# Linear attention and feed-forward kernel: size checks moved ahead of the division, a buffer for the gated row, later weight words, projection banks in the last attention group

## The reference

```python
h = _layernorm(x) * (1 + ca) + sa
x = x + ga * attention(h, W_qkv, b_qkv, W_out, b_out)
h = _layernorm(x) * (1 + cb) + sb
x = x + gb * ffn(h, w_gate, w_up, w_down)

# attention, one row t after the other, per head
q = elu(q * E ** -0.5) + 1.0001
k = elu(k) + 1.0001
kv_s = kv_s + k_t outer v_t
k_s  = k_s + k_t
out_t = (q_t . kv_s) / (q_t . k_s + 1e-6)

# ffn, with integer weights (-127 to 127) times 1/127
h = silu(x @ w_gate.T) * (x @ w_up.T)
return h @ w_down.T
```

## Time and profile before

| What | us |
|---|---|
| median of 3 runs | 2218.9 (2216.57 to 2219.52) |
| profiled execution, whole | 2216.51 |
| its span, first to last instruction | 2214.8 |
| TensorE busy | 2134.8 (96%) |
| VectorE, ScalarE, GpSimd busy | 1212.1, 828.3, 834.9 |
| one pair of attention groups in the loop | 132.5 |
| `out_project`, twelve matmuls, start to start | 2.72 |
| `numerators`, start to end | 2.05 |
| `scores`, `k_turn`, `add_state` | 1.1, 0.43, 0.4 |
| one feed-forward block j, gate and up | 3.63 |
| transposes of group g+1 behind a block | 0.44 |
| TensorE's wait ahead of 69.72, in the first group | 2.33 |

### The profile page before, as it was taken

The page is one execution under the profiler, slowest core; times in us unless marked ns, Lnnn a source line. Parts: engine busy times, 40 slices in busy tenths (PEclk is TensorE's granted clock), DMA queues, the critical chain, the costliest instruction groups (busy, mean ns, idle before and its releaser), DMA issues. The chain is left out here.

```text
span 2214.8 us, 39000 instructions
## 1 busy us (share of the span) xinstructions
PE 2134.8 (96%) x15216; PEld 1746.5 (79%) x15216; DVE 1212.1 (55%) x1702; ACT 828.3 (37%) x1389; POOL 834.9 (38%) x630
## 2 busy tenths in 40 slices
PE   6999999999999999999789999999999999999999
PEld 4788788778778787788678888888888888888887
DVE  7988888888888888888532223322233322333211
ACT  5544444444444444445432233322233212332221
POOL 2633544443544443544333233333333323333333
PEclk9999999999999999999989999999999999999999
DMA  6111211211211211211511100111000111001100
GB/s 242 39 49 49 72 45 59 73 59 58 73 44 61 70 58 63 68 44 58 206 58 39 38 15 25 38 38 38 18 25 33 38 38 38 9 28 38 38 20 20
DMA packets 61079, 117.38 MB, mean 53 GB/s; under 512 B 5137, under 2 KB 5137, under 8 KB 60946
## 3 DMA queue, kind: packets, MB, share of 16 engines
q1 hardware_dynamic: 60418, 114.32, 14.9%
q10 hardware_dynamic: 528, 1.05, 0.1%
HBM read 81.80 MB, written 33.56 MB: 52 GB/s over the span
## 5 line engine op out<-in xcount | busy, mean ns | idle before, releaser
L1203 POOL TENSOR_TENSOR h_lo<-bv_row,h_hi 128x512 fp32r<-128x512 f32 x96 | 124.2, 1293 | 311.3 <-ACT h_hi L1262 311.3
L721 DVE RECIPROCAL r_den<-r_den 128x512 f32<-128x512 f32 x64 | 214.0, 3344 | 0.0
L1203 POOL TENSOR_TENSOR h_lo<-k_sum,h_hi 128x512 fp32r<-128x512 f32 x96 | 123.9, 1291 | 180.4 <-ACT h_hi L1262 180.4
L376 POOL TENSOR_TENSOR x_res<-a_t,x_res 128x512 f32<-128x512 f32 x64 | 81.9, 1280 | 281.3 <-DVE a_t L745 281.2
L1259 ACT ACTIVATE kv_diag<-pj 128x512 f32<-128x512 f32 x96 | 56.5, 588 | 343.3 <-PE pj L1358 343.3
L499 ACT ACTIVATE z_exp<-pj,qk_neg 128x512 f32<-128x512 f32 x128 | 88.1, 688 | 209.5 <-PE pj L958 173.1
L1262 ACT ACTIVATE h_hi<-bv_row 128x512 fp32r<-128x512 f32 x96 | 60.7, 632 | 263.6 <-DVE bv_row L1319 263.6
L726 DVE TENSOR_TENSOR probs<-sc,causal 128x512 f32<-128x512 f32 x256 | 158.4, 680 | 0.9 <-PE sc L986 0.8
L958 PE MATMUL pj<-xt_hi,w_hi 128*128 128x512 f32 x512 | 149.5, 413 | 4.7 <-ACT xt_hi L491 3.5
L1319 DVE TENSOR_TENSOR k_sum<-pj,kv_diag 128x512 f32<-128x512 f32 x96 | 66.4, 692 | 154.5 <-PE pj L1358 116.2
L1370 PE MATMUL num<-wd,h_hi 128*128 128x512 f32 x384 | 149.4, 389 | 0.0
(11 more groups left out here) (172 smaller groups left out, 4934.2 us busy)
## 6 DMA issues: line engine op xcount, KB each, us to landing
x_res<-in_L_attn_x SPq DMA_DIRECT2D x64, 256.0 KB, 2.9
x_mid<-x_res SPq DMA_DIRECT2D x64, 256.0 KB, 2.0
out<-y_rows SPq DMA_DIRECT2D x64, 256.0 KB, 2.0
xg<-in_L_attn_x SPq DMA_DIRECT2D x15, 1024.0 KB, 5.5
word<-in_ffn_words SPq DMA_DIRECT2D x36, 256.0 KB, 2.7
xg<-x_mid SPq DMA_DIRECT2D x9, 1024.0 KB, 5.6
r_den<-x_mid SPq DMA_DIRECT2D x8, 1024.0 KB, 5.7
wd_words<-in_ffn_words SPq DMA_DIRECT2D x12, 256.0 KB, 6.1
```

What stands on the lines that cost most here:

```text
L376: pool.tensor_tensor(out=x_res[:, slot, :], in0=y[:, :], in1=x_res[:, slot, :], op=ALU.add).then_inc(y_ready, 1)
L721: dve.reciprocal(r_den[parity][:, c, :], r_den[parity][:, c, :]).then_inc(rden_ready, 1)
L1203: pool.tensor_tensor(out=h_lo[j], in0=h[j % 2], in1=h_hi[j].bitcast(F32), op=ALU.subtract).then_inc(h_lo_ready, 1)
```

## The change

- `y` is a buffer of its own; `divide` no longer waits for `y_ready`. The two buffers of `word` lie in parts of `r_den`; the first load of a group waits for the divisions of the group before.
- In the loop `word_size` stands ahead of `divide`, and ScalarE waits for the third check behind the last `a_high`.
- The last group's `k_turn` goes to the first bank of `pj` and waits for `v_rows` in place of two masked heads; the projections of tiles 59 to 62 go to the second bank and wait for the gating before.
- SyncE issues the `up` words one tile later, and all of the group-15 words behind the residual load of tile 63, with the feed-forward part's groups 1 and 0 ahead of them (`first_group`). `gb_row` stays behind the last store.
- ScalarE converts the wide words in group 15 only, and the last thirds and the down words inside the first feed-forward group, which is a branch of its own now. TensorE starts that group after 8 conversions and waits for the other 8 at block 8.

The diff's core. The repeats of the `word_size` move at the other two tiles, and lines that pass a name on, are left out.

```diff
@@ -187,8 +188,7 @@
-    y = a_t
-    word = sbuf(s, "word", [P, D])
+    y = sbuf(s, "y", [P, D])
...
@@ -244,14 +244,23 @@
-    silu_row, junk = a_t, word
-    gb_row, ga_sign = a_t, word
+    silu_row, junk = a_t, y
+    gb_row, ga_sign = a_t, y
+    word = [r_den[1 - parity][:, 3, :].bitcast(I32) for parity in range(2)]
+    def turn_bank_of(tile):
+        return pj[:, 0, :] if isinstance(tile, int) and tile >= (NG - 1) * GT else turn_bank
+    def y_bank_of(tile):
+        return pj[:, 1, :] if isinstance(tile, int) and (NG - 1) * GT <= tile + 1 < NG * GT else y_bank
-    def sync(sp):
+    def sync(sp, first_group):
...
@@ -268,10 +277,12 @@
 
-        def load_word(i):
+        def load_word(g, parity, t):
+            i = g * 3 + (t - 6)
+            if t == 0:
+                wait(sp, a_ready, g * GT)
             wait(sp, most_ready, i + 1)
-            sp.dma_start(word[:, :].bitcast(I32), ffn_words[bass.ds(i, 1), :, :].rearrange("a p n -> (a p) n")).then_inc(word_in, 16)
+            sp.dma_start(word[parity], ffn_words[bass.ds(i, 1), :, :].rearrange("a p n -> (a p) n")).then_inc(word_in, 16)
 
...
@@ -324,21 +335,21 @@
+                if isinstance(g, int) and g == NG - 1 and t == 3:
+                    first_group()
+                    load_rest(words_hi, 0, 2)
+                    load_rest(words_lo, HB, 3)
+                    for j in range(HB):
+                        sp.dma_start(wd_words[:, j, :], ffn_words[2 * HB + j, :, :]).then_inc(words_in[4 + j // C], 16)
-                    load_word(g * 3 + (t - 6))
+                    load_word(g, parity, t)
+                if isinstance(g, int) and g == NG - 2 and t == 3:
-                if isinstance(g, int) and g == NG - 1 and t == 0:
-                    sp.wait_ge(pj_ready, NG * UNITS)
-                    load_rest(words_hi, 0, 2)
-                    load_rest(words_lo, HB, 3)
-                    sp.wait_ge(state_ready, (NG - 1) * GT)
-                    for j in range(HB):
-                        sp.dma_start(wd_words[:, j, :], ffn_words[2 * HB + j, :, :]).then_inc(words_in[4 + j // C], 16)
...
@@ -514,7 +525,7 @@
-            act.activation(k_tok[:, :], turn_bank, ACT.Copy).then_inc(ktok_ready, 1)
+            act.activation(k_tok[:, :], turn_bank_of(tile), ACT.Copy).then_inc(ktok_ready, 1)
...
@@ -599,13 +603,13 @@
-            if last:
-                words_to_float(w_lo, words_lo, slice(0, 2 * D), 1)
+            if last:
+                words_to_float(w_hi, words_hi, slice(0, 2 * D), 0)
...
@@ -615,12 +619,12 @@
-            if last:
-                words_to_float(w_hi, words_hi, slice(2 * D, 3 * D), 2)
+            if last:
+                words_to_float(w_lo, words_lo, slice(0, 2 * D), 1)
...
@@ -631,28 +635,23 @@
-            if last:
-                words_to_float(w_lo, words_lo, slice(2 * D, 3 * D), 3)
-                down_to_float(range(0, C))
-            if isinstance(g, int) and g == NG - 2:
-                words_to_float(w_hi, words_hi, slice(0, 2 * D), 0)
-            if last:
-                down_to_float(range(C, HB))
-            else:
+            if not last:
+            if not isinstance(g, int):
+                act.wait_ge(most_ready, g * 3 - 2)
...
@@ -732,7 +731,6 @@
-            wait(dve, y_ready, tile)
...
@@ -742,7 +740,7 @@
-            dve.tensor_tensor(out=y[:, :], in0=y_bank, in1=ga_row[:, :],
+            dve.tensor_tensor(out=y[:, :], in0=y_bank_of(tile), in1=ga_row[:, :],
...
@@ -750,10 +748,10 @@
 
-        def word_size(i, slot):
+        def word_size(i, slot, parity):
 
             wait(dve, word_in, i * 16 + 16)
-            dve.tensor_reduce(most[:, slot:slot + 1], word[:, :].bitcast(I32), AX.X, ALU.max,
+            dve.tensor_reduce(most[:, slot:slot + 1], word[parity], AX.X, ALU.max,
                               apply_absolute_value=True).then_inc(most_ready, 1)
...
@@ -868,9 +866,9 @@
+            if not isinstance(g, int):
+                word_size(g * 3 + (0 - 6), 0, parity)
-            if not isinstance(g, int):
-                word_size(g * 3 + (0 - 6), 0)
...
@@ -988,9 +986,12 @@
         def k_turn(tile, parity, t):
-            wait(pe, probs_ready, tile * HPC + 2)
+            if isinstance(tile, int) and tile >= (NG - 1) * GT:
+                pe.wait_ge(v_ready, NG * C)
+            else:
+                wait(pe, probs_ready, tile * HPC + 2)
             for c in range(C):
-                mm = pe.transpose(turn_bank[:, c * P:(c + 1) * P], kt[parity][:, c, t * P:(t + 1) * P], ident[:, :])
+                mm = pe.transpose(turn_bank_of(tile)[:, c * P:(c + 1) * P], kt[parity][:, c, t * P:(t + 1) * P], ident[:, :])
             mm.then_inc(kt_ps, 1)
...
@@ -1020,11 +1021,13 @@
             wait(pe, a_lo_ready, tile + 1)
-            if not isinstance(tile, int) or tile + 1 < NG * GT:
+            if not isinstance(tile, int) or tile + 1 < (NG - 1) * GT:
                 wait(pe, probs_ready, (tile + 1) * HPC + 1)
+            elif tile + 1 < NG * GT:
+                pe.wait_ge(y_gated, tile)
             passes = [(a, w, c) for a, w in ((a_hi, w_hi), (a_hi, w_lo), (a_lo, w_hi)) for c in range(C)]
             for i, (a, w, c) in enumerate(passes):
-                mm = pe.matmul(y_bank, a[:, c * P:(c + 1) * P], w[:, c, WO:WO + D],
+                mm = pe.matmul(y_bank_of(tile), a[:, c * P:(c + 1) * P], w[:, c, WO:WO + D],
                                start=(i == 0), stop=(i == len(passes) - 1))
...
@@ -1168,14 +1172,13 @@
-        sp.wait_ge(att.a_ready, (NG - 1) * GT)
-        load(0, 0)
-        sp.wait_ge(att.xt_ps, (NG + 1) * C)
-        load(1, 1)
-        sp.wait_ge(att.y_gated, NG * GT)
-        sp.dma_start(gb_row[:, :], gb_dram.broadcast_to([P, D])).then_inc(gb_in, 16)
-        for slot in range(2):
-            sp.wait_ge(att.y_out[slot], 16 * NG * GT // 2)
+        def first_group():
+            sp.wait_ge(att.xt_ps, (NG + 1) * C)
+            sp.wait_ge(att.state_ready, (NG - 1) * GT)
+            sp.wait_ge(att.a_ready, (NG - 1) * GT)
+            load(1, 1)
+            load(0, 0)
...
@@ -1189,9 +1192,16 @@
-        groups(sp, 2, NG - 2, group)
-        for slot in range(2):
-            sp.wait_ge(y_out[slot], 16 * NG * GT // 2)
+        def groups_after():
+            sp.wait_ge(att.y_gated, NG * GT)
+            sp.dma_start(gb_row[:, :], gb_dram.broadcast_to([P, D])).then_inc(gb_in, 16)
+            for slot in range(2):
+                sp.wait_ge(att.y_out[slot], 16 * NG * GT // 2)
+            groups(sp, 2, NG - 2, group)
+            for slot in range(2):
+                sp.wait_ge(y_out[slot], 16 * NG * GT // 2)
+        return first_group, groups_after
...
@@ -1238,20 +1248,19 @@
-        act.wait_ge(att.wide_ready, 1)
-        flag = act.value_load(wide[0:1, 0:1])
-        with act.If(flag > 0):
-            done = 0
-            for first, w in ((0, wg), (HB, wu)):
-                for k in range(C):
-                    for b in range(HID // D):
-                        words(act, ffn_words[first + k * (HID // D) + b, :, :], w[:, k, b * D:(b + 1) * D], done)
-                        done += 1
-            for j in range(HB):
-                words(act, ffn_words[2 * HB + j, :, :], wd[j], done)
-                done += 1
-        def group(g, parity):
+        def words_to_float(w, words, signal):
+            att_words = att.words_in[signal]
+            act.wait_ge(att_words, 16 * C)
+            for k in range(C):
+                act.activation(w[:, k, 2 * D:3 * D], words[:, k, 2 * D:3 * D], ACT.Copy).then_inc(att.gu_ready, 1)
+        def down_to_float(j):
+            act.wait_ge(att.words_in[4 + j // C], 16 * C)
+            act.activation(wd[j], wd_words[:, j, :], ACT.Copy).then_inc(att.wd_ready, 1)
+        def group(g, parity, convert=False):
...
@@ -1262,8 +1271,30 @@
-        groups(act, 2, NG - 2, group)
+                if convert and j in (2, 3):
+                    words_to_float(*((wg, words_hi, 2), (wu, words_lo, 3))[j - 2])
+                if convert:
+                    for i in (range(j - 4, j - 3) if 4 <= j < 8 else range((j - 8) * 3 + 4, min(HB, (j - 8) * 3 + 7)) if j >= 8 else ()):
+                        down_to_float(i)
+        act.wait_ge(att.wide_ready, 1)
+        flag = act.value_load(wide[0:1, 0:1])
+        with act.If(flag < 1):
+            group(0, 0, convert=True)
+        with act.Else():
+            for signal in att.words_in:
+                act.wait_ge(signal, 16 * C)
+            done = 0
+            for first, w in ((0, wg), (HB, wu)):
+                for k in range(C):
+                    for b in range(HID // D):
+                        words(act, ffn_words[first + k * (HID // D) + b, :, :], w[:, k, b * D:(b + 1) * D], done)
+                        done += 1
+            for j in range(HB):
+                words(act, ffn_words[2 * HB + j, :, :], wd[j], done)
+                done += 1
+            group(0, 0)
+        groups(act, 2, NG - 2, group, 1)
...
@@ -1364,7 +1395,7 @@
```

(19 more changed lines are left out.)

18 lines of the change are left out of this document (7 added, 11 removed).

## The result

| | before | after |
|---|---|---|
| median | 2219.2 us (4 runs) | 2196.5 us (4 runs, 2195.5 to 2198.6) |
| profiled execution, its span | 2216.5, 2214.8 | 2196.4, 2194.7 |
| TensorE busy | 2134.8 | 2138.8 |
| VectorE busy | 1212.1 | 1260.3 |

What follows compares the result with a forecast made beforehand. TensorE, busy 2134.8 of 2214.8 us, was taken as the bound, with 80 us idle plus lowered-clock cost to win. 17.5 (loop) + 12 (last group) + 3.5 (first feed-forward group) = 33 off 2218.9: 2185.9 us, range 2178 to 2197.

Steps and rivals of the forecast that it cites:

- 17.5 forecast: Loop and groups without checks: 17.5 of the 17.9 us that TensorE waits for `xf` go; 10 if only the first part worked.
- in its place stands the check, 0.68 for the reduction and about 0.19 for the merge, 0.87: Loop, third tile: the division's 1.56 us wait for `y` goes, the check takes 0.87, so the division comes 0.7 earlier.
- The second rival: Loop: port meetings or other lateness eat the reserve, 13 of the 17.5 us lost; gain 20, 2199 us; chance 0.1.
- the reserve of 0.2: Loop: the read-out of x_bank ends at 918.87, `add_state` at 919.1, so the 1.39 us stall goes with 0.2 us to spare.
- The second part of my gain: Loop, tile before: the check fits into VectorE's 2.15 us idle before the division, and all that follows on VectorE starts 0.87 earlier.
- the signs named for failure: Wrong if `scores` still waits for `xf`, the first turn waits over 4 us, or VectorE waits for a word's DMA.
- 12 forecast: Last attention group: shorter first wait, tile cycle 7.65 for 8.14, long stall gone, less 0.9 for clock; 12 us, bounds 9 and 14.5.
- the 1.1 that I had for `norm_x`: First feed-forward group: 1.1 us more for `norm_x` behind the 3.5 us idle that `gb_row` causes.
- third: Rival: a division waits for its check and so for a late word's DMA; slower, 2225 us; chance 0.03.
- fourth: Rival: the `xf` wait is set by TensorE's own turn, not the division, so little is gained; 2218 us; chance 0.03.
- The fifth: Rival: everything fits better, no cold clock, `gb_row` by 1116; gain 39, 2180 us; chance 0.15.
- 3.5 forecast: First feed-forward group: the wait for `xg` goes, one for `gb_row` comes; 53.8 to 55.5 for 58.1; 3.5 us, bounds -1 and 8.

Runs made afterwards that it cites:

- clamp_late: The changed kernel with the clamp of `gb_row` at block 9 instead of block 1 of the first feed-forward group: 2190.2 us, ratio 0.988.
- words_ahead: The changed kernel with the second and third blocks of weight words issued at tile 0 of group 15, as before the change: 2196.8 us, ratio 0.991.

## Why the prediction was off

**The loop (17.5 forecast, 7.5 measured).** Three things, from rows:
1. The step "in its place stands the check, 0.68 for the reduction and about 0.19 for the merge, 0.87". In the loop it took 1.38, 0.51 more, and the wait shrank by 0.97 where the forecast had the division 1.57 earlier. This leaves the 0.42 and 0.33 in twelve groups: 4.5 us, which the run with the waiting residual won back (5.8). The 0.19 came from rows where the merge ran first: GpSimd's `a_lo` began at 919.86, 0.12 us after it. The second rival had the mechanism, "port meetings", and put the sum at 2199, but it priced it on another instruction and gave it 0.10; and I counted the reserve of 0.2 against sums of 128x512, never asking whether the smallest instruction in the chain could meet one. The row for its neighbour was at hand: the gating's end releases the residual, which starts within 0.2 us (917.00 after 916.86).
2. A wait that was not in the forecast at all: the v of the next group, 0.33 in eleven groups of the loop and 0.4 in group 14, about 4 us (two earlier groups had such a wait before, too). Before, it was decided by 0.02 us:

```profile
936.62 0.69 DVE L693 TENSOR_TENSOR xt_lo<-xf,xt_hi 128x512 fp32r<-128x512 f32 x1 [0.51 <-ACT xt_hi L491]
```

```profile
936.64 1.81 POOL L370 TENSOR_TENSOR x_res<-x_res,gabo_row 128x512 f32<-128x512 f32 x1
```

   `xt_lo` (VectorE) began first and kept its 0.69, and GpSimd's addition took 1.81 instead of 1.27 to 1.29. In the change the addition begins first and `xt_lo` is the one that pays. With the whole check behind the division it is 0.05 us the other way (931.02 GpSimd, 931.07 VectorE): 1.77 for `xt_lo`. The second part of my gain, "all that follows starts 0.87 earlier", holds for GpSimd too, and two engines that move by different amounts can meet.
3. The wait at the loop's turn, 1.9 us, which follows the second.

Added up for the loop: 12x0.97 = 11.6, less about 4 and 1.9, makes 5.7 against 6.0 measured. A pair of groups takes 131.6 (132.6 before, 129.8 forecast). Of the signs named for failure, "scores still waits for `xf`" came true.

**The last group (12 forecast, 10.3 measured).** The pieces: the first turn waited 3.10, not 2.6, since the `xt_lo` ahead of `v` is long (1.33, item 2 again); a tile's cycle 7.75 for 7.65; the other lateness that I had added (0.75 and 0.3) didn't come. The term that was mis-sized is the clock. From the turn to the numerators it took 5.90 (1065.51 to 1071.41); at full clock 3.26 (1084.41 to 1087.67 before), so 2.6 were lost, where I had said 1.4 at most and taken 0.9. Before, the same piece had lost 1.3 (1075.01 to 1079.53). So of the 2.0 us of shorter wait, 1.4 went to the clock. The 7.7 us stall went as forecast, but of the two conditions that I named (the division that doesn't ask for `y`, the words behind residual 63) the words' place did it; with the own `y` alone 6.5 stay.

**The first feed-forward group (3.5 forecast, 2.9 measured).** The stall was right: no wait for `xg`, one for `gb_row`, landing 10.5 us after its issue at 1105.89 (the group began 1096.67), TensorE's stall 3.70 for 3.5, its first down matmul 55.2 after its start, in the range of 53.8 to 55.5. The rest of the sum was right by luck. Without the stall the group takes 48.3 (clamp_late). In the three kernels whose clock stayed full behind it, the stall brought 1.2 more, near the 1.1 that I had for `norm_x`; the 0.9 for a late `h_lo` didn't come; and in the change the clock fell to 0.50 behind the stall and cost 1.9, which no term of the sum had. The Trainium skill (DMA: Bandwidth & Descriptors, Queues, rings and completion order) and its ring order fit both runs: 10.5 us behind the 5 MiB of words and two groups, 3.9 with the words long through.

What I missed is where the clamp stood: the sum priced the wait for `gb_row` and never asked who needs the row. Nobody does before the group's end, and the whole stall with its clock, 6.3 us in the medians, was to be had by changing the block of the clamp. The queue's block of loads is not a fixed point in time, though. It is released by the work of the last attention group, and `gb_row` lands 24.0 to 24.5 us after its first load in six of the seven kernels with this wait, and 25.9 in the seventh. With the merge behind the division that first load comes 6.6 us earlier and `gb_row` 5.2 earlier, and the loop's gain of 5.7 us reaches the total:

```profile
1085.26 0.64 SPq L1181 DMA_DIRECT2D xg<-x_mid  x1
...
1111.14 0.43 DVE L1343 TENSOR_SCALAR z_exp<-ga_row 128x512 f32<-128x512 f32 x1 [9.98 <-DMA ga_row<-gb_dram]
```

Only the words' own move was paid for with this wait: 7.4 us less in the last attention group (42.9 in words_ahead, 35.4 in the change), 6.9 more in the first feed-forward group (48.3 and 55.2).

**The other rivals.** VectorE never waited for a word's DMA (third), and the read-out did follow the division (fourth). The fifth would have needed all of the above to go right; with the merge, the bias addition and the clamp moved, its 2180 is reached: 2177.2.

## What to carry to other kernels

An instruction that is moved into a chain takes its new neighbour's price, not its old one: before taking a duration from a row, look what the other engine does at the new place, and what the same edit moves there. A wait added to an engine with slack, so that it stays out of a short critical stretch, can be worth more than one removed. And a load that is moved out of one stall's way stands in the next one's: the words' move took 7 us out of the last attention group and put as much before the clamp, until the clamp moved too. Ask of every wait that is left who needs its data, and when.

## What was unexpected of the hardware

- A VectorE instruction on 128x1 numbers with two inputs in SBUF took 0.61 to 0.83 us where a GpSimd addition of 128x512 had begun before it, and 0.16 with GpSimd kept idle, or beside an addition that began after it. The Trainium skill (SBUF — State Buffer, Who interferes with whom) says that a VectorE instruction with two SBUF inputs contends with a GpSimd instruction that reads SBUF; that it costs so small an instruction the rest of GpSimd's is what the rows here show. The reduction beside it, with one input, kept its 0.68.
- The same kind of meeting on 128x512 cost `xt_lo` 0.6 to 1.1 us (0.69 alone, 1.32 and 1.77 beside GpSimd), or GpSimd's addition 0.5 (1.81 for 1.27 to 1.29), whichever of the two began later.
- The clock after one and the same wait of 3.1 us: from the turn to the numerators it took 4.58, 4.80 to 4.86 (six kernels), 5.73, 5.90 and 5.92 us, with 3.26 at full clock; 4.85 after 2.47 and 4.52 after 5.11. So the low clock cost 1.3 to 2.7 us, and not by the length of the wait. In the first feed-forward group it stayed full behind waits of 2.98, 3.17 and 3.45 us and fell behind 3.58, 3.70, 4.65 and 4.98. What decides it stays open.
